# Two expert networks: who copies a slot's output out of the banks

## The reference

```python
xn = _layernorm(x)
x = x + _L0_gnn_ref(xn, ...) + _L0_mix_ref(xn[None], ...)[0]
x = x + _L0_ffn_ref(_layernorm(x)[None], ...)[0]     # 8 experts, 2 chosen a node: 768 -> 192 -> 384 -> 768
xn = _layernorm(x)
x = x + _L1_gnn_ref(xn, ...) + _L1_mix_ref(xn[None], ...)[0]
x = x + _L1_ffn_ref(_layernorm(x)[None], ...)[0]     # 8 experts, 2 chosen a node: 768 -> 1152 -> 768
return x
```

```python
for e in range(NE):
    h = _gelu(x @ W1[e] + b1[e])
    h = _gelu(h @ W2[e] + b2[e])      # the second network has no such layer
    y = h @ W3[e] + b3[e]
    out = out + comb[..., e:e + 1] * y
```

## Time and profile before

| | before |
|---|---|
| median of 3 runs | 2485.56 us (2476.71 to 2489.2) |
| the profiled execution | 2478.0 us, its span 2476.3 us |
| TensorE busy | 2178.7 us, 88% |
| VectorE busy | 1413.4 us, 57% |
| ScalarE busy | 945.4 us, 38% |
| GpSimd busy | 505.0 us, 20% |
| first expert network, slots at work | about 1300 to 1455 us |
| second expert network, slots at work | about 2085 to 2450 us |

### The profile page before, as it was taken

The page is one execution under the profiler, slowest core; times in us unless marked ns, Lnnn a source line. Parts: engine busy times, 40 slices in busy tenths (PEclk is TensorE's granted clock), DMA queues, the critical chain, the costliest instruction groups (busy, mean ns, idle before and its releaser), DMA issues. The chain is left out here.

```text
span 2476.3 us, 33659 instructions
## 1 busy us (share of the span) xinstructions
PE 2178.7 (88%) x13261; PEld 2095.4 (85%) x13261; DVE 1413.4 (57%) x2282; ACT 945.4 (38%) x1261; POOL 505.0 (20%) x258
## 2 busy tenths in 40 slices
PE   4899999999999999999958859877778868999994
PEld 4899999999899999999948858777778857999994
DVE  8533355555455224323367866268884676888884
ACT  1222146666333111211126642225512224767672
POOL 4786420000300244334120022211110020000001
PEclk9899999999899999999969979999999978999997
DMA  3412123332323111111048971111122037999995
GB/s 100 135 26 53 58 93 112 128 112 93 138 98 117 39 44 53 58 39 39 14 161 272 315 275 46 64 31 38 44 69 77 14 128 285 349 348 346 357 336 176
DMA packets 158233, 326.83 MB, mean 132 GB/s; under 512 B 14121, under 2 KB 99337, under 8 KB 158091
## 3 DMA queue, kind: packets, MB, share of 16 engines
q1 hardware_dynamic: 133354, 265.68, 31.3%
q10 hardware_dynamic: 18976, 43.33, 4.8%
q0 software_dynamic: 5760, 15.86, 2.1%
HBM read 278.24 MB, written 46.51 MB: 131 GB/s over the span
## 5 line engine op out<-in xcount | busy, mean ns | idle before, releaser
L606 PE MATMUL banks<-weight_hi,xt_hi 128*128 128x384 f32 (+2 forms) x2208 | 738.5, 334 | 69.0 <-DVE xt_lo L1341 15.3
L609 PE MATMUL banks<-weight_lo,xt_hi 128*128 128x384 f32 (+2 forms) x2208 | 722.4, 327 | 0.0
L610 PE MATMUL banks<-weight_hi,xt_lo 128*128 128x384 f32 (+2 forms) x2208 | 722.2, 327 | 0.0
L606 PEld LDWEIGHTS banks<-weight_hi,xt_hi 128*128 128x128 f32 x2208 | 426.5, 193 | 81.3 <-issue 25.6
L609 PEld LDWEIGHTS banks<-weight_lo,xt_hi 128*128 128x128 f32 x2208 | 427.0, 193 | 0.4 <-issue 0.2
L610 PEld LDWEIGHTS banks<-weight_hi,xt_lo 128*128 128x128 f32 x2208 | 426.2, 193 | 0.0
L1766 DVE TENSOR_TENSOR weight_lo<-weight_raw,weight_hi 128x2304 fp32r<-128x2304 f32 (+2 forms) x153 | 342.8, 2244 | 88.5 <-ACT weight_hi L1070 88.5
L1070 ACT ACTIVATE weight_hi<-weight_raw 128x2304 fp32r<-128x2304 f32 (+2 forms) x153 | 287.0, 1880 | 73.1 <-PE banks L606 44.5
L786 POOL TENSOR_TENSOR weight_hi<-weight_raw,zero_col 128x2304 fp32r<-128x2304 f32 (+1 forms) x36 | 119.9, 3331 | 772.6 <-PE banks L606 334.1
L2320 PE MATMUL banks<-held_hi,a_rel 128*128 128x384 f32 x550 | 189.1, 344 | 0.4 <-DVE held_lo L1539 0.4
L2320 PE MATMUL banks<-held_lo,a_rel 128*128 128x384 f32 x550 | 187.6, 341 | 0.0
(11 more groups left out here) (396 smaller groups left out, 3878.1 us busy)
## 6 DMA issues: line engine op xcount, KB each, us to landing
weight_raw<-L_ffn_w_in SPq DMA_DIRECT2D x102, 1152.0 KB, 5.6
weight_raw<-L_gnn_W_in SPq DMA_DIRECT2D x32, 1152.0 KB
weight_raw<-L_ffn_W_in SPq DMA_DIRECT2D x17, 1152.0 KB, 7.5
products<-bias_rows SPq DMA_DIRECT2D x80, 192.0 KB, 1.9
slot_in<-slot_rows ACTq DMA_DIRECT2D x34, 384.0 KB, 6.8
slot_out<-bias_rows ACTq DMA_DIRECT2D x34, 384.0 KB, 5.8
weight_raw<-L_ffn_W_in SPq DMA_DIRECT2D x17, 576.0 KB, 5.8
product_back<-products SPq DMA_DIRECT2D x10, 960.0 KB, 4.7
```

Source lines behind the costliest of these rows:

```text
L606: ins = pe.matmul(dst, s[0], m[0], start=start, stop=False)
L609: pe.matmul(dst, s[0], m[1], start=False, stop=False)
L610: return pe.matmul(dst, s[1], m[0], start=False, stop=stop)
```

## The change

VectorE's `output` is gone, and so is its call ahead of the turn's last `low()`. ScalarE's `rows_out` now makes the two copies itself, with an `Activation` of the function `Copy`, ahead of the store that it begins. The waits on `y_out` and `y_full` move with the copies; `y_used` is raised by ScalarE, and TensorE waits for it as before.

```diff
                 def rows_out(v):
 
+                    if v >= 2:
+                        act.wait_ge(y_out[n][v % 2], 16 * (v // 2))
+                    for c, (bank, cols, width) in enumerate(full_cols(n, last)):
+                        act.wait_ge(y_full[n], 2 * v + c + 1)
+                        act.activation(y_rows[v % 2][:, cols], ps[:, bank, 0:width], ACT.Copy).then_inc(y_used[n], 1)
                     act.wait_ge(y_used[n], 2 * (v + 1))
                     act.dma_start(slot_at(slot_out_dram[n], v), y_rows[v % 2]).then_inc(y_out[n][v % 2], 16)
...
-                def output(v):
-
-                    if v >= 2:
-                        vec.wait_ge(y_out[n][v % 2], 16 * (v // 2))
-                    for c, (bank, cols, width) in enumerate(full_cols(n, last)):
-                        vec.wait_ge(y_full[n], 2 * v + c + 1)
-                        vec.tensor_copy(y_rows[v % 2][:, cols], ps[:, bank, 0:width]).then_inc(y_used[n], 1)
-
...
                         for j in range(parts(n, l)):
-                            if l == last and j == parts(n, l) - 1:
-                                output(v)
                             if l == 0 and j == 0 and v + 1 < XSLOTS:
                                 transposed_lo(0, v + 1)
                             low()
```

## The result

Timed together on one chip, seven executions each, the kernel before has a median of 2485.56 us and the changed kernel of 2469.81 us (2466.69 to 2472.36). The ratio is 0.9942, 95% interval 0.9925 to 0.9959: 14.4 us less of 2485.6, between 10 and 19 (the two medians themselves lie 15.8 apart). The forecast was 9.8 us less, 2475.8.

A forecast was written before the change was run, and what follows sets the result against it. VectorE's two output copies were taken to lie on the path that sets each expert network's turn. Savings of 4.6 (first network), 4.9 (second) and 0.3 us (ends) sum to 9.8, from 2485.6 to 2475.8 us; range 2464 to 2487.

The forecast's parts named there:

- rival B: First network: the DMA does not limit it; 16.2 us saved in all, 2469.4 us; chance 0.27.
- The ring of the first network: First network: a 9.10 us turn is a closed chain through VectorE's two copies; without their 0.93 it leaves 8.17.
- ScalarE itself thus costs 0.08 back: 8.25: First network: with the copies, ScalarE lets the second layer's Gelu begin 0.08 us later, so 8.25 us a turn, saving 0.85.
- The turn of 8.75, held by loads: First network: weight loads keep the turn near the DMA-busy end, saving 0.35 us in 13 turns, 4.6 us.
- The second network: Second network: VectorE's low half behind the copies starts 0.35 us sooner in each of 14 turns, 4.9 us.
- rival D: Both networks: the whole 0.93 us is saved in every turn, 25 us, 2460.5 us; chance 0.03.
- The ends, 0.3 us: End of each network: the last slot's copies take 0.87 in place of 1.02 us, 0.3 us for both.
- Rival E: First network: ScalarE becomes the pace; with copies of 1.4 us each, 1.1 us a turn lost, 2495 us; chance 0.05.

The follow-up runs named there:

- half loads: Changed kernel, loading only the first half of the columns of the third layer's weights in the first network from about its seventh turn on; 2464.04 us.
- the extra copies: Changed kernel with half loads, plus two more copies on ScalarE in each turn of the first network; 2469.18 us.
- the table of who and when: Output copies by VectorE or ScalarE, at the early or late place; against the kernel before, VectorE late 1.0043, ScalarE early 0.9978, changed kernel 0.9942.
- before with half loads: Kernel before, with the same half of the third layer's weight loads left out in the first network; 2481.71 us.
- VectorE's late copies: Changed kernel's late place for the copies, at the start of the next turn, but made by VectorE; 1.0043 of the kernel before.
- the new order: A turn's last high and low half go behind the next turn's hT_hi and hT_lo; three kernels, 0.9896, 0.9877 (0.9898 on another chip) and 0.9908 of before.
- the kernel with rows first in the second network: Changed kernel, with hT_hi and hT_lo ahead of the previous turn's last halves in the second network alone; 2454.36 us, 0.9896 of before.
- The kernel before with rows first: Kernel before, copies still on VectorE, with hT_hi and hT_lo ahead of the previous turn's last halves in both networks; 0.9908 of before.
- the kernel with rows first in both networks: Changed kernel, with hT_hi and hT_lo ahead of the previous turn's last halves in both networks; 0.9877 of before on one chip, 0.9898 on another.

## Why the prediction was right, and where it was off

The time, 2469.8, lies in the range, and all terms have the right sign. The sum was 9.8 us against 14.4 measured by the ratio and 14.2 by GpSimd's two waits. That is outside the forecast's own band, 8 to 12.4 us saved, and inside that of rival B, whose 2469.4 us is almost the measured time. By the mechanism B is wrong all the same: it has 13 x 0.85 = 11.0 us for the first network and 0.3 for the ends, where the measured terms are 7.2 and 2.5. The two misses have opposite signs; that B's number comes so near is luck.

**The ring of the first network.** Right to 0.01 us: 9.10 before, 8.17 in six of the thirteen turns after and in all eight with half loads. The two copies were inside it. That its terms add up to 9.10 "with no gap" is no evidence: they are differences of successive start times from one turn to the next, and such a sum always closes. What makes it a ring is that every step is either work or a wait with its releaser in the earlier trace rows, and what proves it is the 9.10 - 0.93 = 8.17 measured.

**"ScalarE itself thus costs 0.08 back: 8.25."** Wrong. The forecast let ScalarE's work behind the copies keep its place; but the first `Gelu` had stood behind VectorE's copies and a store, and came 0.17 us sooner with the copies on ScalarE: 1364.82 - 1361.09 = 3.73 us after the large low half's start, before 1386.79 - 1382.89 = 3.90. That is more than 0.08. The turns with half loads have the same 3.73 and are 8.17. And a delay there would have been shared over two turns, as the extra copies showed.

**The turn of 8.75, held by loads.** The mechanism is shown by the half loads; the size was off. It is 8.55: 0.55 x 13 = 7.2 us in place of 4.6. The error is in the reading of "busy": 9.10 x 0.97 = 8.83 took the busy time of a turn as fixed, and put the guess near it. It is not fixed: after the change a turn has 8.55 x 0.99 = 8.46 of it for the same bytes (311 x 9.10 = 2.83 MB, 327 x 8.55 = 2.80 MB). The same bytes, asked for in a shorter turn, took 0.37 us less of busy time. The rate of the second network, 350 GB/s, was not reached either; the truth lay about midway between the ends, 8.25 and 8.83, and the 8.75 chosen between them was a guess that fell too near one end.

**The second network.** 0.35 a turn forecast, 0.32 measured (a mean turn of 22.48 to 22.16, the wait from 1.23 to 0.91), 14 x 0.32 = 4.5 in place of 4.9. The low half does start at once behind ScalarE's high half and no sooner, which rules out rival D; and the table of who and when shows that this gain a turn owes nothing to ScalarE's being the one that copies.

**The ends, 0.3 us.** Mis-sized: 7.0 - 4.5 = 2.5 us in the second network; in the first, 7.2 - 7.2 leaves nothing. The forecast forgot that in the last turn no high half is behind the copies: there VectorE's whole 0.93 was on TensorE's path. Its last wait for `hT_lo`, before:

```profile
2436.09 0.56 PE L606 MATMUL banks<-weight_hi,hT_hi 128*128 128x384 f32 x1 [3.38 <-DVE hT_lo L1776]
```

and after:

```profile
2432.65 0.41 PE L606 MATMUL banks<-weight_hi,hT_hi 128*128 128x384 f32 x1 [2.39 <-DVE hT_lo L1781]
```

0.99 us less. The rest is TensorE's clock. The last slot from its predecessor's store to its own, before:

```profile
2434.63:2448.01 13.38, 11.29 (x54) 10.99 (x54) 2.38 (x5) 0.00 (x0) 0.00 (x0) 0.87 0.07 29
```

and after:

```profile
2431.69:2442.93 11.24, 9.72 (x54) 9.43 (x54) 0.85 (x2) 0.96 (x2) 0.00 (x0) 1.00 0.09 35
```

The same 54 matmul records took 11.29 and 9.72 us, at a mean granted clock of 0.87 and 1.00: 1.57 us. (The store is begun at another point of the turn, so the lengths of the two stretches are not compared.)

**Rival E.** ScalarE did not become the pace; 0.86 to 0.88 us for a pair, as counted.

The sum with measured sizes: 7.2 + 4.5 + 2.5 = 14.2.

## What to carry to other kernels

A ring in which every step has its work or its releaser tells what is won by taking work out of it; that its sum closes tells nothing. The time that the DMA engines are busy does not tell what the next limit will be, because it can shrink (8.83 to 8.46 us a turn here for the same bytes); a kernel that leaves out half of a load does. When an edit moves work both to another engine and to another time, run the two other combinations: here one network's gain came from the engine and the other's from the time. And before work is moved away from behind a wait, see whether the waiting item can be put ahead of it: the order was worth 15 us more of the second network's wait (399.4 to 384.2), some 11 us more of the whole by the ratios, and left the move itself 0.1 to 0.3%.

## What the runs showed of the hardware that was not expected

TensorE's granted clock at the edges of a stage differed between kernels and executions. In one execution of each, in the last slot of the second network it was 0.87 before and with the change in the first network only, 0.77 before with half loads, 0.85 with VectorE's late copies, and 1.00 in all five kernels in which ScalarE makes the second network's copies in the old order of the halves; so far as single executions tell, it went with the kernel, and 1.6 us of the gain with it. With the new order it was 0.87 in all three kernels. The wait ahead of it was 3.38 us before and 2.39 after. That a shorter wait kept the clock up is a guess, and the kernel with rows first in the second network speaks against it: a wait of 2.4 and yet 0.87. Why it stays up is open.

The first slots of the first network ran at 0.50 of full speed, which is the lower level of 1.2 GHz, for some 19 us from TensorE's first transpose of a slot in the profiles of before and after, and for some 9 us in those of three of the experiments (the change in one network only, either one, and the changed kernel with half loads). From that transpose to the second large low half it took 28.3 to 28.4 us in the first two and 25.3 to 25.5 in the three; this is the 3 us between "wait 1" of the changed kernel, 170.4, and that of the kernel with the change in the first network only, 167.9, whose turns are the same. It did not follow the kernel: the change in the second network only leaves this network as it was before.

Over 200 us the DMA engines moved more than the 350 GB/s of before. The kernel before with rows first, second network:

```profile
2200.00:2400.00 200.00, 200.00 (x1203) 199.30 (x1202) 175.88 (x125) 150.72 (x133) 0.00 (x0) 1.00 1.01 373
```

373 GB/s, above the 358 that the Trainium skill's page "DMA: Bandwidth & Descriptors", section "Where 436 GB/s comes from", gives for a core's share of HBM and from which rival B was argued; the same section has 425 GB/s for a 16 MB transfer, and here, with one core at work, the measurement decides. The trace of before had been above 358 as well, in slices of 5 us: those of 2200 to 2400 us run from 210 to 413 GB/s, so its 350 was a mean over uneven demand. The first network, whose loads come in more and smaller pieces, stayed at 321 to 327 GB/s at a busy share of 0.99 to 1.00 in the changed kernel and the two with rows first in both networks.

In one execution of the kernel with rows first in both networks the matmuls were slow: 11589.86 us against 2448.72 to 2454.27 in the other four. One of the page's costliest groups of that execution, and of the kernel with rows first in the second network:

```profile
L609 PE MATMUL banks<-weight_lo,xt_hi 128*128 128x384 f32 (+2 forms) x2208 | 2764.9, 1252 | 0.0
```

```profile
L609 PE MATMUL banks<-weight_lo,xt_hi 128*128 128x384 f32 (+2 forms) x2208 | 723.1, 327 | 0.0
```

1252 ns a matmul in place of 327, with a granted clock of 1.000 in the record, while VectorE's low halves took 2246 ns in the mean as against 2245. So the granted clock did not show what slowed TensorE here; the cause is open. One of twelve executions of the kernel with the change in the second network only was slow in another way, 3183.29 us against 2467.30 to 2480.81, and there the granted clock did show it: a mean of 0.645 in place of 0.943 to 0.950.
